# A two-layer mixture of experts on one core: 64 fixed places per expert in two strips, and overflow tokens as a list of 32-token units

## The reference

```python
# layer 0: expert e has its own hidden width, top 2 of 8 by softmax
HID0 = [432, 528, 624, 752, 896, 1088, 1312, 1584]
for e in range(NUM_EXPERTS):
    w = jnp.sum(jnp.where(idx == e, val, 0.0), axis=-1)
    g = x_flat @ gates[e].T
    u = x_flat @ ups[e].T
    h = jax.nn.silu(g) * u @ downs[e].T
    out_flat = out_flat + w[:, None] * h
...
# layer 1: eight experts of hidden width 768 with biases, top 2 of 8
for e in range(E):
    h = jax.nn.relu(xr @ w1[e].T + b1[e])
    y = h @ w2[e].T + b2[e]
    out = out + tok_w[:, e:e + 1] * y
```

## Time and profile before

| what | value |
|---|---|
| runs | 212.15, 1023.98, 213.1 us; median 213.1 |
| profiled execution | 212.31 us, span 210.2 us |
| granted TensorE clock | 1.0 over the span |
| TensorE busy | 194.4 us, 92% of the span |
| VectorE, ScalarE, GpSimd busy | 102.0, 66.6, 40.1 us |
| moved by DMA | 33.55 MB |

### The profile page before, as it was taken

One profiled execution on the slowest core, in us unless ns is written; L12 is line 12 of the kernel. 1 busy time (PEld: TensorE's weight loads), 2 busy tenths in 40 slices (PEclk: granted clock), 3 DMA queues, 4 the chain that ended last, 5 costly groups with the idle time before them and its releaser, 6 DMA issues.

```text
span 210.2 us, 5352 instructions
## 1 busy us (share of the span) xinstructions
PE 194.4 (92%) x2257; PEld 132.6 (63%) x2257; DVE 102.0 (49%) x284; ACT 66.6 (32%) x152; POOL 40.1 (19%) x65
## 2 busy tenths in 40 slices
PE   7799899998899999999999979898898999999992
PEld 7679777567546555545455768665586465575791
DVE  0342786747813431121121425978478579746431
ACT  2243587727222221221322325578351000000010
POOL 1413400003995000000000003000017970000000
PEclk9999999999999999999999999999999999999999
DMA  6999999994100000000000199999300000510001
GB/s 202 391 433 434 434 414 441 440 431 142 54 3 3 0 3 3 0 3 0 3 8 2 26 366 438 417 421 423 164 0 2 3 0 3 164 63 3 3 0 45
DMA packets 4989, 33.55 MB, mean 160 GB/s; under 512 B 664, under 2 KB 2144, under 8 KB 2656
## 3 DMA queue, kind: packets, MB, share of 16 engines
q1 hardware_dynamic: 4384, 32.37, 37.8%
q10 hardware_dynamic: 576, 0.79, 1.2%
HBM read 32.95 MB, written 0.20 MB: 158 GB/s over the span
## 4 chain that ended last, share of the span: by engine, by line
PE 79%; DVE 8%; issue 5%; ACT 3%; DMA 2%; POOL 2%; DVEq 0%; POOLq 0%
PE bank L1498 14%; PE bank L1443 13%; PE bank L1458 8%; PE bank L1250 5%; PE bank L1418 4%; PE bank L1205 4%; PE bank L1132 4%; PE bank L1471 3%; PE bank L1361 3%; PE bank L1262 3%; PE bank L1164 3%; PE bank L1234 3%; PE bank L1480 2%; DMA x<-x_dram 2%; PE bank L1179 1%
## 5 line engine op out<-in xcount | busy, mean ns | idle before, releaser
L1498 PE MATMUL bank<-w,scratch 128*32 128x192 f32 x648 | 30.1, 329 | 0.7 <-ACT scratch L598 0.7
L1443 PE MATMUL bank<-w,scratch 128*32 128x512 f32 (+3 forms) x332 | 30.6, 492 | 0.0
L1498 PEld LDWEIGHTS bank<-w,scratch 128*32 128x32 f32 x648 | 19.1, 109 | 15.4 <-issue 7.1
L929 DVE TENSOR_TENSOR scratch<-scratch,bank 128x512 f32<-128x512 f32 (+1 forms) x12 | 7.9, 655 | 37.1 <-ACT scratch L607 37.1
L1132 PE MATMUL bank<-ones 128*128 128x128 f32 x162 | 23.4, 297 | 1.7 <-POOL ones L508 1.4
L1132 PEld LDWEIGHTS bank<-ones 128*128 128x128 f32 x162 | 21.4, 208 | 2.8 <-POOL ones L508 1.4
L516 POOL TENSOR_TENSOR rstd<-var_eps,minus_half 128x2 f32<-128x2 f32 x4 | 2.8, 710 | 104.0 <-DVE var_eps L760 104.0
L563 POOL TENSOR_SCALAR scratch<-const,place,gate 128x96 f32<-128x96 f32 x32 | 22.1, 707 | 0.5 <-issue 0.4
L690 ACT ACTIVATE scratch<-bank,neg_max 128x256 f32<-128x256 f32 x48 | 19.7, 480 | 7.9 <-DVE neg_max L823 7.7
L1443 PEld LDWEIGHTS bank<-w,scratch 128*32 128x32 f32 x332 | 11.2, 110 | 11.3 <-issue 8.9
L1458 PE MATMUL bank<-w,scratch 64*32 64x512 f32 (+3 forms) x332 | 17.8, 497 | 0.0
(11 more groups left out here) (178 smaller groups left out, 264.9 us busy)
## 6 DMA issues: line engine op xcount, KB each, us to landing
w<-experts_dram SPq DMA_DIRECT2D x9, 1152.0 KB, 18.1
w<-experts_dram SPq DMA_DIRECT2D x1, 3624.0 KB, 41.5
w<-experts_dram SPq DMA_DIRECT2D x1, 3024.0 KB, 23.7
w<-experts_dram SPq DMA_DIRECT2D x1, 2496.0 KB, 33.4
w<-bias_slots_dram SPq DMA_DIRECT2D x1, 2304.0 KB
w<-experts_dram SPq DMA_DIRECT2D x1, 2016.0 KB, 28.0
w<-experts_dram SPq DMA_DIRECT2D x1, 1704.0 KB, 17.0
w<-experts_dram SPq DMA_DIRECT2D x1, 1416.0 KB, 12.4
```

Source lines behind the costliest of these rows:

```text
L1443: nc.tensor.matmul(first_bank(m, which)[rows, to:to + wide], xe_hi[:, e, tokens_at(q, i)], w0[:, at:at + wide], start=col == 0, stop=False ...
L1498: last = nc.tensor.matmul(y_bank_of(layer, i)[UNIT * q:UNIT * (q + 1), 0:C], hT[:, col, UNIT * q:UNIT * (q + 1)], w0[:, at:at + C], start= ...
```

## The change

Each expert now has 64 fixed places, and the array is split into two strips of 64 columns: `SIDES` says which experts each side works through, two side by side. Layer 0 has 30 blocks per side, 8 macro steps, the last of two blocks; layer 1 has 24, 4 macro steps. `GROUPED` pairs the sides' outputs for the combines, five in layer 0 and four in layer 1, in place of six and six; the rounds of turned weights are three and two, in place of three each. The gather is one batch of 512 columns for each half of the channels, in place of two of 384, and the rest of the rounding moves from GpSimd to VectorE.

Tokens beyond the 64th of an expert are cut into units of 32. An **item** is one unit with one part of its expert's weights: in layer 0 four blocks (an expert has 1, 2, 2, 2, 2, 3, 3 or 4 such parts), in layer 1 the whole expert. Four items make a **job macro step**, one in each strip of 32 columns, in the same form as a macro step of before. Both layers have them now, up to 11 and 3; the extra passes, the transposed jobs and their lists are gone. With the given inputs there are 8 items in layer 0 and 7 in layer 1, two job macro steps each.

The list of items is made in macro step 0, in both layers: VectorE counts the candidates, TensorE adds them up over the partitions, VectorE lists them, TensorE spreads the list, and VectorE writes the numbers for the registers. All engines branch on the number of job macro steps (`job_macros`), in nested branches whose bodies are written out for each number.

```diff
-WIDE = ((1, 2, 3, 4, 5, 7), (2, 3, 4, 5, 6, 7))
-NARROW = ((0, 0, 0, 6, 6, 6), (0, 0, 0, 1, 1, 1))
+STRIP = 64
+SIDES = (((7, 6, 3), (5, 4, 2, 1, 0)), ((0, 2, 4, 6), (1, 3, 5, 7)))
+GROUPED = (((0, 0), (None, 1), (1, 2), (None, 3), (2, 4)), tuple((i, i) for i in range(E // 2)))
...
+        def job_macros(eng, layer, n, iteration, drain):
...
+                elif k == 0:
+                    with eng.If(n > 1):
+                        iteration(0, True)
+                        rest(1)
+                    with eng.Else():
+                        iteration(0, False)
+                        drain(1)
...
+                        for q in range(QUADS):
+                            at, free = ROOMS[layer][k % 2][q]
...
+                            item = sp.value_load(job_regs[0:1, 1 + QUADS * k + q:2 + QUADS * k + q], min_val=0,
+                                                 max_val=(OFFP0[E] if layer == 0 else E) - 1)
+                            if free > 0:
+                                sp.wait_ge(main[layer]["down_done"], free)
+                            of = (items0, experts1)[layer][:, bass.ds(item, 1), :].rearrange("p e c -> p (e c)")
+                            sp.dma_start(w0[:, at:at + ROOM], of).then_inc(job_landed[layer][k], 16)
...
+            def number_slots(layer):
+
+                sems, n = main[layer], ITEMS[layer]
+                dve.wait_ge(sems["slots_psum"], 1)
+                step(nc.vector.tensor_copy(slot_of[:, :, 0:n], bank[6][:, 0:3 * n].rearrange("p (a k) -> p a k", a=3)))
+                step(nc.vector.tensor_copy(job_regs[0:1, 0:1], job_number[0:1, :]))
+                nc.vector.tensor_copy(job_regs[0:1, 1:1 + n], slot_of[0:1, 2, 0:n]).then_inc(sems["jobs_ready"], 1)
...
+            def iteration(layer, m, prepared=None):
+
+                sems = main[layer]
+                first_upper(layer, m)
...
+                for g in range(GROUPS[layer] + JOB_MACROS[layer]):
+                    if combined_at(layer, g) == m:
+                        combine(layer, g)
+                if prepared is not None:
+                    gather_job(layer, prepared)
+                first_lower(layer, m)
+                if m == 0:
...
+                    nc.tensor.matmul(out_ap, ones[:], cand_slots[:, :, 0:n], start=True, stop=True).then_inc(sems["slots_psum"], 1)
+                    pe.wait_ge(sems["jobs_ready"], 1)
+                else:
+                    down(layer, m - 1)
```

More of the change, by code:

```diff
@@ L1393, in combine @@
-            def combine(layer, sems, e, turned, first, last):
-                pe.wait_ge(sems["y_ready"], e + 1)
-                for t in range(TT):
-                    ins = nc.tensor.matmul(bank[4][:, t * C:(t + 1) * C], turned[0:SLOTS, t * P:(t + 1) * P], y_out[0:SLOTS, e % 2, :],
-                                           start=first and t == 0, stop=last, skip_group_check=True)
-                ins.then_inc(sems["combined"], 1)
             def turn_weighted(layer, round_):
-                pe.wait_ge(weighted_ready, TT * E * layer + weighted_count(round_))
+                pe.wait_ge(weighted_ready, weighted_count(layer, round_))
@@ L1446, in first_lower @@
             def first_lower(layer, m):
[L1448 to L1455 removed]
+                if m == 0:
+                    pe.wait_ge(xe_vec, layer + 1)
@@ new lines, in drain @@
+            def drain(layer, k):
+                m = MACROS[layer] + k - 1
+                turn_hidden(layer, m)
+                left = [g for g in range(GROUPS[layer] + k) if combined_at(layer, g) > m]
+                for g in left:
+                    if combined_at(layer, g) == m + 1:
+                        combine(layer, g)
+                down(layer, m)
+                if layer == 0:
+                    keep_clock(KEEP_SUM)
+                for g in left:
+                    if combined_at(layer, g) > m + 1:
+                        combine(layer, g)
+                if layer == 0:
+                    keep_clock(KEEP_NORM)
@@ L1510, in experts @@
+            def experts(layer):
+                pe.wait_ge(xn_rounded, layer + 1)
+                for c in range(2):
+                    gather(bank[2 + c][:], c, lambda t: chosen[:, t].rearrange("p e s -> p (e s)"), TT * layer).then_inc(xe_psum, 1)
                 if layer == 1:
```

1042 lines of the change are left out of this document (467 added, 575 removed).

## The result

The changed kernel takes 215.47 us (median of four runs, 214.29 to 215.81) against 212.62 before: a ratio of 1.0131, 95% interval 1.0072 to 1.019. The forecast was 204.2 with a range to 210. Medians are of all executions; a ratio goes by those in the faster of the two states that executions fall into, so it can differ from the quotient of the medians. The macro steps did become fewer and no dearer; what they gave was spent mainly on one wait for transfers and on a clock that the forecast had kept out of its sum.

The account below looks back on a forecast made before the run. The prediction took TensorE's own work in the expert stages as the bound. Macro steps −6.25 and −4.85, starts −3.1, list wait +5.2, loads +0.9, jump 0 made −8.1 from 212.31: 204.2 us, range 200.5 to 210.

Parts of the forecast that it names:

- The macro steps: Both layers' expert stages: fewer steps at the same price, two job steps each; −6.25 us in layer 0, −4.85 in layer 1.
- rival C: Macro steps: two strips of 64 do not run side by side, so products cost twice; +39, 243 us; chance 0.04.
- The start and the wait for the list: Stage starts earlier, together −3.1 us; TensorE's wait for the job list before step 1, 2.6 per layer, +5.2.
- The fetched weights: Job loads: hidden in layer 0; in layer 1 the eighth lands late for the second job step, +0.9 us.
- the lesser lateness of rival B: Layer 1's job loads late, but not enough for a slower kernel: 206.5 to 215 us; chance 0.10.
- rival B: Layer 1's eight job loads, issued by a register's number, come late; chance 0.10 for lesser lateness, 0.03 for slower.
- Rival B's case of 4.1 us a load: Layer 1's eighth job load lands at 202.3, 9.9 late: 213 us, no gain.
- its case of 5.2: Layer 1's job loads served one by one, the eighth 16.3 us behind its step: 219.6 us, slower.
- The clock: Gaps of 2 us, new in the expert stages, let the granted clock fall for some us; counted only among rivals.
- rival A: Layer 0's jump comes 2.7 us late or gaps lower the clock: 2.5 to 5 more, 206.7 to 209; chance 0.15.
- The jump: Taken branch at the end of layer 0's drain, over bodies of longer lists: 0 us, or 2.7 late behind the fillers.

Follow-up runs that it names:

- the run with the late wait and no rows: Changed kernel with TensorE's wait for the list moved behind step 1's first products and layer 1's bias rows not fetched: 205.09 us, 0.9633.
- the late wait: Changed kernel with TensorE's wait for the list moved behind step 1's first products in both layers: 213.17 us, 1.0006.
- the fillers: Changed kernel with 13 filler products of 128 columns ahead of TensorE's wait for the list in both layers, the wait kept: 218.44 us, 1.0199.
- the missing rows: Changed kernel without fetching the eight bias rows of layer 1's job steps: 207.57 us, 0.977.
- the kernel before with a gap: Kernel before the change, with three chained VectorE copies that TensorE must wait for before step 1 in both layers: 215.73 us, 1.0161.
- the repaired kernel: Changed kernel with the list wait behind step 1's first products and each layer 1 job load cut in two halves: 203.9 us, 0.96.
- the five edits that keep them: Changed kernel, each alone: no bias rows 207.57 us; room for two job steps 214.97; halved loads 208.07; spread rows 213.16; short rows 209.94.

## Why the prediction was wrong

Against the profiled execution of 214.29 the forecast of 204.2 is 10.1 short. By its own steps:

*The macro steps* were right. Layer 0 from step 1 to its last combine is 54.16 us, 52.6 without the 1.6 that the clock took, as forecast; layer 1 is 45.74, less 5.28 and 3.2 for wait and clock 37.3 against 36.8. A plain step took 4.77 where four strips took 4.76. Two strips of 64 cost what four of 32 did; rival C is out.

*The start and the wait for the list* were nearly right in layer 0 (first upper products at 55.12 against 55.1, step 1 at 60.74 against 60.6), and some 0.6 short in layer 1. What the forecast did not see is that the wait need not be on the path: moved behind step 1's first products it is 0.22 us.

*The fetched weights* are the first of the two steps that failed: +0.9, between 0 and +2, measured 5.28. The forecast took the bias rows as 96 KB more at the rate of the loads before, which had no such rows among them (in their slices the row reads 417 to 438 GB/s, not 421 to 441, which changes little). Without rows that rate holds (420 to 427 GB/s), with them it is 352 to 369 in the same view. This was the lesser lateness of rival B, by another mechanism than the one it named: not the register, but the rows. Shown by taking them out. The rows are not all of it: from the first load's issue to the last landing the forecast allowed 26.2 us, where the changed kernel took 31.7 up to the step that waits; without rows it would have allowed 24.4, where the run with the late wait and no rows took 26.4. (Rival B's case of 4.1 us a load has the 2.4 of the start in it, its case of 5.2 has not; reckoned alike, 4.1 is 7.5 late, not 9.9.)

*The clock* is the other step that failed. It had no term in the sum, since fillers stand around the jump and a gap comes once per layer; it stood in rival A at 0.15, as an alternative to the forecast. It came on top: 1.6 and 1.3 us behind the waits for the list, 1.9 behind the wait for the loads, 4.8 together. That it goes with the waits is shown by the late wait, the fillers and the missing rows, each of which removes the slow stretch at its place. A gap of that length alone need not do it, as the kernel before with a gap shows.

*The jump* was taken at 0 between 0 and 2.7. The branch does lie beside the fillers, from 0.30 behind the combine, but the kernels without it are 0.55 to 0.91 faster there. Against the forecast's 3.47 only 0.3 of it shows.

Together: 4.4 for the loads, 4.8 for the clock, 0.3 for the longer way from the last combine to the normalisation (3.81 against 3.47), 0.6 for layer 1's start, 0.1 for layer 0's and 0.4 for layer 1's steps, less 0.5 behind the last combine: 10.1. That the median of the repaired kernel, 203.9, stands near the forecast is in part luck: its two edits take away the two terms that were missing, but also the two waits for the list (3.1 us), which the forecast had in its sum, and its two fastest runs take 201.8 and 202.5.

What stays open: why the clock fell behind some gaps and held behind others of the same length. Of the twelve gaps of 1.5 to 2.1 us before step 1 in the traces of the changed kernel and of the five edits that keep them, it fell behind ten. Before the second job step it fell behind a wait of 2.61 us and held behind one of 2.77, both behind full products.

## What to carry to other kernels

Price a new transfer by its shape and by what it queues among, not by its bytes alone: here 8% more bytes, onto 32 partitions at a time, made the whole queue some 15% slower. Ask of each new wait of the bounding engine how late it may stand: the list was waited for ahead of products that make no use of it, and one half of the second job step's weights is needed some 7 us after the other. When a change brings TensorE to a stand, put the slow restart, with its odds, into the sum, not only among the rivals, and remember that a wait which hides a second one passes its gain on to it.

## What the runs showed of the hardware that was not expected

A taken branch on TensorE's queue took 3.33 to 3.87 us, 22 times of 23 in the traces (once 1.41), where one not taken took 65 to 89 ns. The granted clock held at 1.0 through gaps of 1.92 and 1.62 us, and once of 2.77, behind full products, and went to 0.50 behind one of 1.21 us that followed thin ones. In the kernel with both repairs the DMA engines were busy at as little as 251 GB/s while transfers of 96 KB onto 32 partitions went among the loads, beside 410 without them. In the changed kernel such transfers made the weight packets queued beside them last 415 ns in place of 360; the same bytes spread over 128 partitions did not (365).
